# Pair products of a CIN tower: one field rotation by transfers into cycles and replicas, against base tiles loaded from e transposed, wide products, and G in one native matmul

## The reference

```
e = stack(tbl_f[ids[:, f]])                              # (2048, 39, 16)
for W in (W0, W1):                                       # W0: 128 x 39*39, W1: 128 x 128*39
    inter = x[:, :, None, :] * e[:, None, :, :]          # x is e at first, then the layer's output
    x = einsum('bid,hi->bhd', inter.reshape(B, -1, 16), W)
    outs.append(x.sum(axis=-1))                          # sum over d: 128 numbers
h = concatenate([outs[0], outs[1], dense_ctx])           # 272
y = relu(relu(h @ W_top1 + b_top1) @ W_top2 + b_top2) @ W_top3
```

## Time and profile before

| | us |
|---|---|
| median of 3 runs | 967.51 (964.41 to 972.47) |
| span of the profiled execution | 1508.4 |
| GpSimd busy in it (628 instructions) | 623.7 |
| TensorE, VectorE, ScalarE busy in it | 884.9, 648.8, 600.9 |

### The profile page before, as it was taken

The page is one execution under the profiler, slowest core; times in us unless marked ns, Lnnn a source line. Parts: engine busy times, 40 slices in busy tenths (PEclk is TensorE's granted clock), DMA queues, the critical chain, the costliest instruction groups (busy, mean ns, idle before and its releaser), DMA issues.

```text
span 1508.4 us, 15925 instructions
## 1 busy us (share of the span) xinstructions
PE 884.9 (59%) x3824; PEld 686.1 (45%) x3824; DVE 648.8 (43%) x1012; ACT 600.9 (40%) x1033; POOL 623.7 (41%) x628
## 2 busy tenths in 40 slices
PE   0136393719268292763958367291863936629998
PEld 0014262508146181552846256270642724527886
DVE  2015292617155282442835156160632615427870
ACT  0013282407154171532735154160532714418772
POOL 6756437461714517154271715417054071450000
PEclk9997596759678596785977678595775967859999
DMA  4112142212122132122322122121221312203320
GB/s 130 24 39 61 38 113 52 69 45 66 26 75 61 23 98 68 38 52 51 85 59 58 27 77 71 39 67 25 78 59 18 95 27 70 67 13 101 106 78 3
DMA packets 101439, 88.81 MB, mean 59 GB/s; under 512 B 59925, under 2 KB 71325, under 8 KB 101250
## 3 DMA queue, kind: packets, MB, share of 16 engines
q1 hardware_dynamic: 81410, 83.02, 18.8%
q0 software_dynamic: 19968, 5.15, 3.9%
HBM read 21.35 MB, written 10.49 MB: 21 GB/s over the span
## 4 chain that ended last, share of the span: by engine, by line
PE 38%; another core or an unknown queue 28%; issue 20%; ACT 6%; DVE 4%; POOL 2%; DMA 1%; DVEq 0%; ACTq 0%; SPq 0%; POOLq 0%
PE mlp_ps L440 7%; PE g_ps L429 6%; PE x_ps L400 5%; PE x_ps L397 5%; PE x_ps L398 5%; PE rep_ps L386 3%; POOL e_rows L346 2%; ACT G L589 2%; PE mlp_ps L471 2%; PE mlp_ps L459 2%; DVE products L739 2%; ACT product_hi L572 2%; DVE product_lo L748 1%; PE aux_ps L368 1%
## 5 line engine op out<-in xcount | busy, mean ns | idle before, releaser
L346 POOL DMA_INDIRECT e_rows<-in_tbl_dram,ids_sb x624 | 623.5, 999 | 721.3 <-DMA ids_sb<-in_ids_dram 535.7
L748 DVE TENSOR_TENSOR product_lo<-products,product_hi 117x512 fp32r<-117x512 f32 (+1 forms) x448 | 308.1, 688 | 598.7 <-remote 369.6
L572 ACT CAST product_hi<-products 117x512 fp32r<-117x512 f32 (+1 forms) x448 | 281.4, 628 | 298.7 <-remote 131.2
L400 PE MATMUL x_ps<-product_lo,w_hi 117*128 117x512 f32 (+1 forms) x448 | 199.3, 445 | 176.0 <-issue 91.8
L397 PE MATMUL x_ps<-product_hi,w_hi 117*128 117x512 f32 (+1 forms) x448 | 254.7, 569 | 9.9 <-issue 9.9
L589 ACT COPY G<-g_ps 128x320 f32 (+1 forms) x256 | 189.4, 741 | 38.2 <-remote 24.6
L400 PEld LDWEIGHTS x_ps<-product_lo,w_hi 117*128 117x128 f32 (+1 forms) x448 | 92.5, 207 | 224.1 <-issue 104.5
L398 PE MATMUL x_ps<-product_hi,w_lo 117*128 117x512 f32 (+1 forms) x448 | 190.3, 425 | 0.0
L429 PE MATMUL g_ps<-e_diag,x1T_hi 128*128 128x320 f32 x512 | 134.7, 347 | 92.6 <-issue 58.9
L440 PE MATMUL mlp_ps<-G,w1T 128*128 (+1 forms) x624 | 186.8, 400 | 0.8 <-ACT G L589 0.8
L429 PEld LDWEIGHTS g_ps<-e_diag,x1T_hi 128*128 128x128 f32 x512 | 97.6, 206 | 126.9 <-issue 82.7
(11 more groups left out here) (42 smaller groups left out, 612.7 us busy)
## 6 DMA issues: line engine op xcount, KB each, us to landing
shifted<-cycle SPq DMA_DIRECT2D x128, 234.0 KB
left<-cycle SPq DMA_DIRECT2D x192, 78.0 KB
e_scratch<-e_parts SPq DMA_DIRECT2D x16, 640.0 KB
e_diag<-e_scratch SPq DMA_DIRECT2D x512, 20.0 KB
e_rows<-in_tbl_dram,ids_sb POOLq DMA_INDIRECT x624
shifted<-cycle SPq DMA_DIRECT2D x64, 156.0 KB
w1T<-in_L_rec_W_dram SPq DMA_DIRECT2D x1, 2496.0 KB
G<-in_L_rec_W_dram SPq DMA_DIRECT2D x1, 819.0 KB
```

Source lines behind the costliest of these rows:

```text
L346: nc.gpsimd.indirect_dma_start(out=e_rows[slot][:, f * D:(f + 1) * D], out_offset=None, in_=tables[f], in_offset=bass.IndirectOffsetOnAxis ...
L400: last = nc.tensor.matmul(x1_ps[c % 2][:, :], w0_hi[0:rows, k, :], product_lo[0:rows, (c * KT + k) % LO_RING, :], start=False, stop=(k == ...
L572: nc.scalar.copy(product_hi[0:rows, n % RING, :], products[0:rows, n % RING, :]).then_inc(hi_ready, 1)
L748: nc.vector.tensor_tensor(product_lo[0:rows, n % LO_RING, :], products[0:rows, n % RING, :], product_hi[0:rows, n % RING, :].bitcast(f32), ...
```

## The change

- **Shifts.** Five base tiles of e transposed (`bases`, each of up to three blocks of 39 rows beginning at chosen fields) hold all shifts: 7 pairs of them give 7 pieces. Sync loads the 14 blocks from `eT` for two chunks (64 rows, 1024 columns) at a time. Replication by TensorE, `cycle`, `left` and `shifted` are gone.
- **Wide products.** The 7 pieces are multiplied in 4 groups of 2, 2, 2 and 1, so products, rounding and lower parts are instructions of 1024 elements (one of 512). Every piece has its own slot, for one chunk.
- **e as it is.** VectorE copies e twice into `e_d` (one copy a tile, no split), native transposes follow, and the store for G takes 40 of 79 numbers of each (row, d).
- **G** is one native float32 matmul for each of the 4 parts; x1 transposed isn't split.
- **One tile per batch.** Layer 1 and MLP work on 128 rows, spread over the steps of the next two tiles. The loops are written out.
- **Gathers.** All ids come in two loads at the start, rows have three slots, and VectorE takes up tile t+1 in chunk 0 of tile t.
- Weights of layer 1 are laid out by transfers from ScalarE's queue at the start.

```diff
+STARTS = ((0, 0, 0), (1, 2, 3), (6, 12, 7), (31, 23, 22))
+MIXED = (0, 13)
+BASES = STARTS + (MIXED,)
+PAIRS = ((0, 1), (0, 2), (0, 3), (0, 4), (1, 2), (1, 3), (2, 3))
+GROUPS = ((0, 1, 2, 0), (0, 3, 2, 2), (1, 2, 2, 4), (2, 3, 1, 6))
+LAYER1 = ((5, 4, 0, 0), (0, 2, 2, 2), (2, 2, 2, 2), (4, 4, 4, 4))
...
+            def store_e(t):
+                sp.wait_ge(e_d_ready, t + 1)
+                sp.dma_start(rows_scratch[t * TB:(t + 1) * TB, :, :], e_d[:, :, F:2 * F + 1]).then_inc(e_stored, 16)
+
+            def load_bases(u):
+                sp.wait_ge(eT_ready, (u // 2 + 1) * ET)
+                after(sp, product_ready, (u - 1) * 2 * NG)
+                half = eT[:, :, :].rearrange("r b d -> r (b d)")[:, u % 2 * HALF:(u % 2 + 1) * HALF]
+                for a, starts in enumerate(BASES):
+                    for n, start in enumerate(starts):
+                        sp.dma_start(bases[u % 2][n * F:(n + 1) * F, a, :],
+                                     half[start:start + F, :]).then_inc(bases_ready[u % 2], 16)
...
+            sp.dma_start(ids_sb[:, 0:1, :], tile_ids[:, 0:1, :]).then_inc(ids_loaded[0], 16)
+            sp.dma_start(ids_sb[:, 1:TILES, :], tile_ids[:, 1:TILES, :]).then_inc(ids_loaded[1], 16)
...
+            for g in range(CHUNKS):
+                t, c = divmod(g, CPT)
+                if g % 2 == 0 and g // 2 + 1 < HALVES:
+                    load_bases(g // 2 + 1)
+                spread(g)
+                if c == 1 and t + 1 < TILES:
+                    store_e(t + 1)
+                if c == 0 and t >= 3:
+                    store_y(t - 3)
...
+            for t in range(TILES):
+                if t <= 1:
+                    pool.wait_ge(ids_loaded[t], 16)
+                after(pool, e_d_ready, t - E_SLOTS + 1)
+                for f in range(F):
+                    nc.gpsimd.indirect_dma_start(
+                        out=e_rows[t % E_SLOTS][:, f * D:(f + 1) * D], out_offset=None, in_=tables[f],
+                        in_offset=bass.IndirectOffsetOnAxis(ap=ids_sb[:, t, f:f + 1], axis=0),
+                    ).then_inc(gathered[t % E_SLOTS], 16)
...
-                for n, (x, part) in enumerate(((x1T_hi, 0), (x1T_hi, 1), (x1T_lo, 0))):
-                    last = nc.tensor.matmul(g_ps[q % 2][:, :], x[:, q, :], e_diag[c % 2][:, :, q, part, :],
-                                            start=(n == 0), stop=(n == 2))
+                nc.tensor.matmul(g_ps[q % 2][:, :], x1T[:, q, :], e_diag[g % 2][:, :, q, :],
+                                 start=True, stop=True).then_inc(e_diag_free if q == Q - 1 else g_in_ps, 1)
...
+            def copy_e(t):
+                dve.wait_ge(gathered[t % E_SLOTS], (t // E_SLOTS + 1) * 16 * F)
+                after(dve, eT_in_ps, ET * t)
+                after(dve, e_stored, 16 * t)
+                rows = e_rows[t % E_SLOTS][:, :].rearrange("b (n f d) -> b d n f", n=1, d=D)
+                nc.vector.tensor_copy(e_d[:, :, 0:2 * F].rearrange("b d (n f) -> b d n f", f=F),
+                                      rows.to_broadcast([TB, D, 2, F])).then_inc(e_d_ready, 1)
+
+            def multiply(g, n):
+                a, b, count, first = GROUPS[n]
...
+                dve.wait_ge(bases_ready[u % 2], (u // 2 + 1) * 16 * LOADS)
+                after(dve, lo_ready, (g - 1) * NG + n + 1)
+                nc.vector.tensor_tensor(products[:, first:first + count, :], bases[u % 2][:, b:b + count, cols],
+                                        bases[u % 2][:, a:a + 1, cols].to_broadcast([R, count, COLS]),
+                                        ALU.mult).then_inc(product_ready, 1)
+
+            def lower_parts(g, n):
+                _, _, count, first = GROUPS[n]
+                dve.wait_ge(hi_ready, g * NG + n + 1)
+                after(dve, contracted, (g - 1) * NG + n + 1)
+                nc.vector.tensor_tensor(product_lo[:, first:first + count, :], products[:, first:first + count, :],
+                                        product_hi[:, first:first + count, :].bitcast(f32), ALU.subtract).then_inc(lo_ready, 1)
...
```

More of the change, by code:

```diff
@@ L25 @@
 H = 128
[L26 to L29, removed]
+KT = (F + 1) // 2
+ROWS = F
+CYCLE = F
+FO = F + 1
 TB = 128
@@ L68, in after @@
-def after(engine, semaphore, value):
[L70 to L96, removed]
@@ L99, in rep_before @@
[L99 to L115, removed]
+GAP = 32
+E_SLOTS = 3
+STARTS = ((0, 0, 0), (1, 2, 3), (6, 12, 7), (31, 23, 22))
+MIXED = (0, 13)
@@ new lines, in cin_tower @@
+        e_rows = [sb(f"e_rows{n}", [128, F * D]) for n in range(E_SLOTS)]
+        e_d = sb("e_d", [128, D, 2 * F + 1])
+        eT = sb("eT", [2 * F, TB, D])
+        bases = [sb(f"bases{n}", [R, len(BASES), HALF]) for n in range(2)]
+        products = sb("products", [R, NT, COLS])
+        product_hi = sb("product_hi", [R, NT, COLS], f32r)
+        product_lo = sb("product_lo", [R, NT, COLS], f32r)
+        x1 = sb("x1", [H, COLS])
+        x1T = sb("x1T", [128, Q, H])
+        e_diag = [sb(f"e_diag{n}", [128, QB, Q, FO]) for n in range(2)]
@@ new lines, in round_products, with copy_x1 @@
+            def round_products(g, n):
+                _, _, count, first = GROUPS[n]
+                act.wait_ge(product_ready, g * NG + n + 1)
+                after(act, contracted, (g - 1) * NG + n + 1)
+                nc.scalar.copy(product_hi[:, first:first + count, :], products[:, first:first + count, :]).then_inc(hi_ready, 1)
+            def copy_x1(g):
+                act.wait_ge(contracted, (g + 1) * NG)
+                after(act, x1T_in_ps, g)
+                nc.scalar.copy(x1[:, :], x1_ps[g % 2][:, :]).then_inc(x1_ready, 1)
@@ new lines, in copy_y @@
+            def copy_y(t):
+                act.wait_ge(y_in_ps, t + 1)
+                after(act, y_stored, 16 * t)
+                nc.scalar.copy(y[:, :], mlp_ps[0:1, 2, :]).then_inc(y_ready, 1)
+            act.wait_ge(zeroed, 1)
+            for row, k, j, shift, count in runs:
+                halves = 1 if shift == 0 else 2
+                act.dma_start(w0_both[row:row + count, 0:halves, k, :],
+                              w0[j:j + count, 0:halves, shift, :]).then_inc(w0_loaded, 16)
@@ L654, in _ @@
             for n in range(ET):
-                copy_eT(0, 0, n)
+                copy_eT(0, n)
+            round_products(0, 0)
             act.wait_ge(mlp_loaded, 5 * 16)
-            copy_cycle(0, 0)
-            round_product(0, 0, 0)
-            for c in range(CPI):
-                chunk(0, c, first=True)
-            for c in range(CPI):
-                chunk(1, c, second=True)
-            with act.Fori(2, ITERS - 1) as it:
-                for c in range(CPI):
-                    chunk(it, c)
@@ L786, in _ @@
-            split_hi(0, 0, 0)
-            split_lo(0, 0)
-            multiply(0, 0, 0)
-            for c in range(CPI):
-                chunk(0, c, first=True)
-            with dve.Fori(1, ITERS - 1) as it:
-                for c in range(CPI):
-                    chunk(it, c)
-            end = ITERS - 1
-            for c in range(CPI):
-                chunk(end, c, final=True)
-            lower_x1T(end, CPI - 1)
-            lower_dense(end)
+            dve.wait_ge(dense_loaded, 16 * 3 * GAP // D)
```

710 lines of the change are left out of this document (269 added, 441 removed).

## The result

The changed kernel takes 1072.3 us (median of 4 runs, 1069.9 to 1073.9), the kernel before on the same chip 970.0: ratio 1.107, 95% interval 1.103 to 1.112. It is slower, as forecast, by 10.7% where 6.5% was forecast.

What follows compares the result with a forecast made beforehand. GpSimd's gathers were taken to bound the kernel: 783 us of gathers, 1.4 + 1.5 + 83 + 1 + 24 behind them make 894, plus 137 of holds is 1031 us, 6.5% slower; range 940 to 1125.

Steps and rivals of the forecast that it cites:

- The bound: In the kernel before, GpSimd's 39 gathers a tile at 1.25 us take 48.8 us, more than compute; ids cause no waits.
- holds: Time a gather stands because of VectorE: 75 us in the kernel before, 137 us forecast after the change.
- tail: After the last gather: 1.4 landing, 1.5 copy, 83 for 7.5 chunks, 1, and 24 drain, giving 894 us plus holds.
- Compute hidden below: Per-tile work of the other engines: 46 us before, 44 after, under the gathers' 49, so not seen while gathers run.
- the sum: Changed kernel: 783 us of gathers plus landing, copy, chunks and drain make 894 us, to which holds are added.
- rivals 1 and 2: Ids waits explain the 75 us, 904 to 934, chance 0.20; wait per gather stays 0.16, 951 or 965, chance 0.20.
- The wide instructions: A gather meeting VectorE's two-SBUF-input instructions waits for their end; 1024 elements take 1.227 us, average wait 0.47 us before correction.
- p: Start-to-start interval of gathers beside compute: 1.41 us before, 1.60 us after the change, own range 1.5 to 1.8.
- the 626 us of compute beside gathers: Changed kernel: 14.1 tiles of 44.4 us run beside gathers, the time to which holds apply, giving 137 us.
- Sync: Its queue takes 47 us a tile with 8 for the 160-byte store of e, under the 57 of gathers.
- Rival 3: Gathers starve (p between 1.8 and 2.28) or sync's 160-byte store takes 16 us or more: 1085 to 1177 us; chance 0.13.
- Rival 4: Each gather holds VectorE's next two-input instruction for up to 0.94 us, 81 us a tile, 1376 us; chance 0.02.

Runs made afterwards that it cites:

- one-input reduction: Changed kernel with each product and lower part replaced by a VectorE reduction over one element of one input: 957.3 us, ratio 0.990.
- The copies: Each product and lower part with two SBUF inputs replaced by a VectorE copy: changed kernel 1265.0 us, ratio 1.301; kernel before 1073.7 us, ratio 1.111.
- 512 columns: Changed kernel with each wide product and lower part issued as one VectorE instruction per 512 columns: 960.5 us, ratio 0.995.

## Why the prediction was right, and where not

**The bound: right.** GpSimd's gathers at 1.25 us bound the kernel before, ids didn't. The kernel before profiled again has 72 us of holds for 75, a tail of 110.5 for 109.8, and loading ids ahead changes nothing.

**Compute hidden below: wrong.** This is the step that failed, and the forecast felt it twice, in the holds and in the tail. I read 46 us a tile from three chunks behind the last gather. Those chunks contain no transposes and copies of e, which come once a tile and make one chunk 13 to 15 us long; compute alone takes 49.4. For the change I took 44.4 and it takes 51.2. TensorE saves four replications a chunk (0.23 us from start to start each, 3.7 us a tile), but G's native matmul takes 0.54 us where three reduced ones took 0.44, layer 1 has twice as many matmuls, and G waits for e_diag behind the loads. I can't add these parts up to the difference; only the totals are measured. In the changed kernel gathers take about 59 us a tile and cover all of it. But had the holds gone, the sum would have said 894 + 14 and the chip says 957: rivals 1 and 2, with 904 to 965 us, mostly lay below what the kernel can do.

**The wide instructions: right in mechanism, and p right, by luck in part.** They took 1.22 us where 1.227 was worked out and 0.69 where 0.688. Gathers start within and end 0.82 us after them. The prediction asked for gathers of about 1.3 us beside compute, 1.6 from start to start. From each copy of e to VectorE's next wait for rows, 444 gathers of the changed kernel take 1.29 us in the mean and start every 1.60 us. So p = 1.60 is what the trace shows (and 1.38 in the kernel before profiled again, for 1.41). What was too small is the other factor, the 626 us of compute beside gathers. These stretches last 687 us without the waits for bases, 49.6 us a tile in the thirteen full ones behind the second, for 44.4. 687 x (1 - 1.25/1.60) = 150 us of holds, 13 more than forecast; the remaining 12 of the 162 lie outside the stretches and in rounding.
That p came out right is luck in part, since two pieces of its estimate were off in opposite directions. I had a gather held by any instruction running 0.12 us after its start. But those that began from 0.04 us before its start on hardly ever hold it in the changed kernel and its variants, which gives fewer places to be held. And I had averaged over a random start, but gathers don't start at random: one that has been released meets the next wide instruction but one at its beginning. The upper end in the text, "a gather released at one end, then held to the end of the second wide instruction after it", is this, and 72 gathers do it, each with a pitch of 2.27, nearly half of the holds (73 us of 166 in the records). Splitting the instructions took away 112 us of time; lengthening them by 5% took away 44.

The Trainium skill (SBUF — State Buffer, Who interferes with whom) names a VectorE instruction with two SBUF inputs as one that contends with GpSimd's reads. With products as they are 162 us of holds agree, and 14 us with the one-input reduction. It also names copies and casts in a mode that uses both ports for one tensor, and gives the lock to whoever comes first for one whole instruction. The copies held gathers indeed, 356 us of holds, although they took 1.10 us for 1024 elements, little less than the products' 1.21. "For one instruction" is not what every gather shows: 8.49 and 10.30 us are ten instructions in a row. The page also infers that descriptor generation needs only the write interface, so that products with two inputs wouldn't hold it; here, where GpSimd reads ids from SBUF for each transfer, they do.

**Tail.** After the last gather came 124.6 us where 1.4 + 1.5 + 83 + 1 + 24 = 111 were forecast: 3.35 until the copy of e for 1.4, 91.4 us from there to the last copy of x1 for 85.5 (the chunk of 15.6 again), 29.9 of drain for 24. These 14 us and the 25 of the holds are 39 of the 41 us between 1031 and 1072; the rest lies around the span. The too short tile of compute accounts for 13 of the 25 and for about 6 of the 14.

**Sync.** The store of 160-byte pieces took 0.6 us in its queue's row (median of 16) for 8 assumed; when its bytes have landed that row doesn't say. The loads took 13.2 to 14 us for 11.2. Rival 3's cost by sync wasn't there while gathers decide; when they don't, its queue is what a misplaced wait stops.

**Rival 4** is out: products beside held gathers take 1.21 us as elsewhere.

**The profile.** "The new profiled span should again be far above the median" was wrong: the late results of the earlier trace rows belonged to one execution. Planning for runs without them was right, though only the sum spoke for it then. What made them late stays open.

## What to carry to other kernels

When GpSimd issues indirect transfers, look at the length and pitch of VectorE's instructions against a transfer's own cycle, not at how busy VectorE is: here 14 instructions of 0.69 us beat 8 of up to 1.22, and 1080 elements beat 1024. Take the price of hidden compute from a stretch that holds every part of a tile's work, or run the kernel with the bound thinned out; the tail flatters it. And when a forecast's product comes out wrong, measure each factor before one of them is blamed: here the start-to-start time was right and the time it applied to was not. And before moving a waiting transfer ahead of another in a queue, ask what stands behind it.

## What the runs showed that I had not expected

- A gather met by back-to-back VectorE work can be held for ten instructions (8.49 us with copies, 10.30 with products), and once for 22 (13.63 us, 512 columns). Why most are let go at the end of one instruction and some only at a pause isn't settled.
- One execution of a kernel under the profiler took 1508.4 us and the next one 966.4, with the same instructions.
- An undisturbed gather takes 0.94 us. A held one ends 0.82 us after the VectorE instruction that held it (the median of each of the twelve profiles without copies in place of products), with copies mostly 0.11 to 0.12 us after it.
